# Low-rank products of a fused adaLN-FFN in three fp32r passes, their factors split by GpSimd, and two output tiles between z and the close

## The reference

```python
q = quantise(x)                      # 8 threshold groups, 64 levels, dequantised again
gates = softmax over the top 2 of 4 of (q @ router_w.T)
x = x + sum_e gates[e] * 4 * (q @ A[e].T) @ B[e].T          # 4 experts of rank 16
y = x @ W.T + 0.5 * (x @ lora_A[label[b]]) @ lora_B_w.T      # rank 32, one of 5 per batch
z = y @ kernel + bias + (y @ A_eff[b].T) @ B_eff[b].T + (y @ A_shared.T) @ B_shared.T
return x + z                         # A_eff, B_eff: 16 adapters mixed by gate[b], rank 32
```

## Time and profile before

| | |
|---|---|
| three timed runs | 505.6, 509.23, 509.37 us, median 509.23 |
| the profiled execution | 506.32 us, its span 504.5 us |
| busy: PE, weight load, DVE, ACT, POOL | 468.8, 407.4, 393.5, 364.7, 7.8 us |
| mean granted TensorE clock | 0.992 of 2.4 GHz |
| matmul records | 2968 |

### The profile page before, as it was taken

How to read it: one execution, slowest core, us unless ns; L and a number is a source line. 1 busy time by engine, 2 the same in 40 slices (tenths; PEclk the granted TensorE clock), 3 DMA queues, 4 the chain that set the end, 5 groups by cost and what they waited for, 6 DMA issues and landing times.

```text
span 504.5 us, 7250 instructions
## 1 busy us (share of the span) xinstructions
PE 468.8 (93%) x2968; PEld 407.4 (81%) x2968; DVE 393.5 (78%) x380; ACT 364.7 (72%) x330; POOL 7.8 (2%) x12
## 2 busy tenths in 40 slices
PE   3779998997798999999999999999999799989897
PEld 3654786786566888789898998998998798978896
DVE  0596578977998989949769989799699993899610
ACT  4856977857679579765779799795899778579002
POOL 0000000001000001000000000000000000000000
PEclk9999999999899999999999999999999989999999
DMA  8955641212432236410413414312413103101102
GB/s 289 388 212 164 221 137 53 54 51 53 135 94 56 70 119 149 168 46 1 129 30 124 146 54 125 106 53 73 149 61 128 48 24 127 53 2 42 43 1 83
DMA packets 36082, 51.24 MB, mean 102 GB/s; under 512 B 27058, under 2 KB 27314, under 8 KB 33650
## 3 DMA queue, kind: packets, MB, share of 16 engines
q1 hardware_dynamic: 34898, 42.40, 26.6%
q0 software_dynamic: 1152, 8.39, 4.6%
HBM read 40.03 MB, written 10.49 MB: 100 GB/s over the span
## 4 chain that ended last, share of the span: by engine, by line
PE 62%; DVE 18%; ACT 10%; issue 7%; DMA 2%; ACTq 0%; DVEq 0%; POOLq 0%
PE bank L887 11%; PE bank L889 11%; PE bank L888 11%; DVE val L572 7%; PE bank L899 5%; PE bank L807 5%; PE bank L781 4%; ACT val L381 4%; DVE val L555 3%; ACT level L370 3%; DVE inside L565 3%; PE bank L846 2%; PE bank L850 2%; PE bank L847 2%; PE bank L803 2%
## 5 line engine op out<-in xcount | busy, mean ns | idle before, releaser
L887 PE MATMUL bank<-x_hi,p_hi 128*128 128x256 f32 x512 | 154.4, 302 | 0.0
L381 ACT ACTIVATE val<-level,shift,par 128x2048 f32<-128x2048 int16 x64 | 133.9, 2092 | 21.0 <-DVE val L572 21.0
L889 PE MATMUL bank<-x_hi,p_lo 128*128 128x256 f32 x512 | 145.1, 283 | 0.0
L888 PE MATMUL bank<-x_lo,p_hi 128*128 128x256 f32 x512 | 145.1, 283 | 0.0
L572 DVE COPY_PREDICATED val<-inside,val 128x2048 f32<-128x2048 uint8 x56 | 141.9, 2534 | 0.3
L370 ACT ACTIVATE level<-xq,inv 128x2048 int16<-128x2048 f32 x64 | 127.8, 1997 | 0.4
L555 DVE TENSOR_SCALAR val<-val,width,unshift 128x2048 f32<-128x2048 f32 x64 | 86.2, 1348 | 40.5 <-ACT val L381 40.0
L887 PEld LDWEIGHTS bank<-x_hi,p_hi 128*128 128x128 f32 x512 | 98.3, 192 | 5.7 <-issue 4.6
L888 PEld LDWEIGHTS bank<-x_lo,p_hi 128*128 128x128 f32 x512 | 98.4, 192 | 1.1
L889 PEld LDWEIGHTS bank<-x_hi,p_lo 128*128 128x128 f32 x512 | 98.3, 192 | 0.0
L565 DVE TENSOR_SCALAR inside<-absx,thr 128x2048 uint8<-128x2048 f32 x56 | 71.3, 1286 | 1.8 <-ACT absx L362 1.8
(11 more groups left out here) (83 smaller groups left out, 470.0 us busy)
## 6 DMA issues: line engine op xcount, KB each, us to landing
xq<-xt_in POOLq DMA_DIRECT2D x8, 1024.0 KB, 5.9
wst<-w_in SPq DMA_DIRECT2D x16, 512.0 KB, 3.5
xs<-xt_in SPq DMA_DIRECT2D x8, 1024.0 KB, 6.3
out_t<-ost SPq DMA_DIRECT2D x16, 512.0 KB, 3.0
la<-la_in SPq DMA_DIRECT2D x4, 512.0 KB, 7.2
kst<-k_in SPq DMA_DIRECT2D x4, 512.0 KB, 12.7
lb<-lb_in SPq DMA_DIRECT2D x1, 2048.0 KB, 21.7
kst<-k_in SPq DMA_DIRECT2D x1, 2048.0 KB, 8.0
```

The lines of the kernel that those rows point to most:

```text
L381: nc.scalar.activation(val[:, turn(c, g)], level[:, g % 2], ACT.Relu, bias=shift[:, g:g + 1], scale=par[:, 1, g:g + 1]).then_inc(raised, 1)
L887: mm(o, p_hi[:, h, k, at:at + P], x_hi[:, s, k], start=k == 0, stop=False)
L888: mm(o, p_hi[:, h, k, at:at + P], x_lo[:, s, k], start=False, stop=False)
L889: mm(o, p_lo[:, h, k, at:at + P], x_hi[:, s, k], start=False, stop=False)
```

## The change

- **Three passes for z.** bu_product (bet*ub, unchanged, fp32) is now a function of its own, and z_begin is 8 times three fp32r matmuls, ub_hi*x_hi + ub_hi*x_lo + ub_lo*x_hi, with the x_hi and x_lo that the tiles use. So it waits for x_lo and ub_lo. The place is behind tile j = 5 (ZAT), where it was 4; for batch 0 z_begin stands behind the products of bet with P (L867 to L869), where it was ahead of them.
- **Three passes for each close.** tb_hi*z_hi + tb_hi*z_lo + tb_lo*z_hi in place of tb*zt.
- **GpSimd splits for each batch.** adapters_split: ub_hi and ub_lo, 128x512 each; z_split: z_hi and z_lo, 128x256 each. In its order adapters_split(b+1) stands ahead of z_split(b). ub has one buffer instead of two, and SP's adapters(b) waits for the split and the bu product of the batch before.
- **The rows of tb are split once.** DVE makes t_lo (8 instructions of 64x512), the two v_lo rows and two bp_lo rows; the lo part of t goes through DRAM too; ACT writes the bp rows once (2 instructions less), and two DMAs copy them to the second slot.
- **The xq loads** go from POOL's queue to ACT's.
- **The schedule.** z_end(z) follows tile ZEND[z], now q = 5, 13, 21, 30, 41, 50, 61 for batches 1 to 7, and the close follows two tiles later where six banks allow it: CLOSE is q = 0, 8, 16, 24, 32, 43, 52, 61 (before 0, 8, 16, 24, 32, 41, 50, 61). XAT is (0, 2), was (1, 3).

```diff
+    XAT, ZAT = (0, 2), 5
+    MID, RANK, GATE, TURN, OUT_AT = {}, {}, {}, {}, []
+    ZEND, CLOSE = [], []
     for c, d in enumerate(DONE):
         mid_at, rank_at, gate_at, turn_at, out_at = LAGS[c]
         MID[d + mid_at], RANK[d + rank_at], GATE[d + gate_at], TURN[d + turn_at] = c, c, c, c
-
-        OUT[d + out_at if c < ZSLOTS else max(d + out_at, STEPS + (c - ZSLOTS + 1) * KT)] = c
-    OUT = {c: at for at, c in OUT.items()}
-    OUT_AT = OUT
-    OUT = {at: c for c, at in OUT_AT.items()}
-
-    XAT, ZAT = (1, 3), 4
-
-
-    CLOSE = [0 if OUT_AT[b] < STEPS + b * KT else max(1, OUT_AT[b] - STEPS - b * KT) for b in range(BATCH)]
-
-    ZOUT = [b * KT + (CLOSE[b] + 1 if CLOSE[b] else 0) for b in range(BATCH)]
+        OUT_AT.append(max(d + out_at, STEPS + ZEND[c - ZSLOTS] + 2 if c >= ZSLOTS else 0))
+
+        ZEND.append(max(OUT_AT[c] - STEPS, (c - 1) * KT + ZAT))
+        CLOSE.append(min(max(ZEND[c] + 2, c * KT), c * KT + CRING - 1))
+        assert CLOSE[c] >= ZEND[c]
+    OUT = {at: c for c, at in enumerate(OUT_AT)}
+    ZOUT = [0] + [z + 1 for z in ZEND[1:]]
     LAG = 2
-    TAKE = [max(q + LAG, ZOUT[q // KT]) for q in range(BATCH * KT)]
+    TAKE = [max(q + LAG, CLOSE[q // KT] + 1) for q in range(BATCH * KT)]
...
-            for c in range(BATCH):
-                if c == 1:
-                    pool.wait_ge(bw_in, 16)
-                if c >= 2:
-                    pool.wait_ge(levels_made, (c - 1) * G)
-                    pool.wait_ge(abs_made, c - 1)
-                pool.dma_start(xq[:, c % 2], x_v[c]).then_inc(xq_in[c % 2], 16)
+            def adapters_split(b):
+                pool.wait_ge(ub_in, 32 * (b + 1))
+                if b:
+                    pool.wait_ge(z_read, b)
+                nc.gpsimd.tensor_copy(ub_hi, ub).then_inc(ub_hi_made, 1)
+                pool.wait_ge(ub_hi_made, b + 1)
+                nc.gpsimd.tensor_tensor(ub_lo, ub, ub_hi.bitcast(F32), ALU.subtract).then_inc(ub_lo_made, 1)
+
+            def z_split(b):
+                pool.wait_ge(zt_made, b + 1)
+                pool.wait_ge(mgt_made, b + 1)
+                if b >= 2:
+                    pool.wait_ge(ofull, STEPS + (b - 1) * KT)
+                nc.gpsimd.tensor_copy(z_hi[:, b % 2], zt[:, b % ZSLOTS]).then_inc(z_hi_made, 1)
+                pool.wait_ge(z_hi_made, b + 1)
+                nc.gpsimd.tensor_tensor(z_lo[:, b % 2], zt[:, b % ZSLOTS], z_hi[:, b % 2].bitcast(F32), ALU.subtract).then_inc(z_lo_made, 1)
+
+            adapters_split(0)
+            for b in range(BATCH):
+                if b + 1 < BATCH:
+                    adapters_split(b + 1)
+                z_split(b)
...
-                sp.dma_start(t_dram[g * RG:(g + 1) * RG].rearrange("r b d -> (r b) d"), tst[0:2 * R, g % 2]).then_inc(t_stored[g % 2], 16)
+                sp.dma_start(t_dram[0][g * RG:(g + 1) * RG].rearrange("r b d -> (r b) d"), tb_hi[0:2 * R, g % 2].bitcast(F32)).then_inc(t_stored[g % 2], 16)
+                sp.wait_ge(t_lo_made, 2 * (g + 1))
+                sp.dma_start(t_dram[1][g * RG:(g + 1) * RG].rearrange("r b d -> (r b) d"), t_lo[:, g % 2].bitcast(F32)).then_inc(t_stored[g % 2], 16)
 
             def adapters(b):
-                s = b % 2
-                sp.dma_start(ub[:, s, :, 0:R], u_dram[b]).then_inc(ub_in[s], 16)
-                sp.dma_start(ub[:, s, :, R:2 * R], a["al"][bass.ds(label[b], 1)].rearrange("o p k r -> p (o k) r")).then_inc(ub_in[s], 16)
+                if b:
+                    sp.wait_ge(ub_lo_made, b)
+                    sp.wait_ge(bufull, b)
+                sp.dma_start(ub[:, :, 0:R], u_dram[b]).then_inc(ub_in, 16)
+                sp.dma_start(ub[:, :, R:2 * R], a["al"][bass.ds(label[b], 1)].rearrange("o p k r -> p (o k) r")).then_inc(ub_in, 16)
...
             sp.wait_ge(w_hi_made, STEPS)
             sp.wait_ge(w_lo_made, STEPS)
             sp.dma_start(bet, a["bet"]).then_inc(bet_in, 16)
             sp.wait_ge(ofull, STEPS - 1)
             sp.dma_start(xs, x_v[0]).then_inc(xs_in, 16)
+            adapters(1)
 
             def xs_load(b):
                 sp.wait_ge(x_lo_made, b * XPARTS)
-                sp.wait_ge(z_read, b)
                 sp.dma_start(xs, x_v[b]).then_inc(xs_in, 16)
-                if b + 1 < BATCH:
-                    adapters(b + 1)
-
+
+            sp.wait_ge(bp_made, HALVES)
+            sp.wait_ge(bp_lo_made, HALVES)
+            sp.dma_start(tb_hi[2 * R:P, 1].bitcast(F32), tb_hi[2 * R:P, 0].bitcast(F32)).then_inc(bp_moved, 16)
+            sp.dma_start(tb_lo[2 * R:P, 1].bitcast(F32), tb_lo[2 * R:P, 0].bitcast(F32)).then_inc(bp_moved, 16)
             xs_load(1)
             for b in range(BATCH):
                 for h in range(HALVES):
...
                     sp.dma_start(out_t[b, :, half], ost[:, half]).then_inc(out_stored[h], 16)
                     if h == 0 and b + 2 < BATCH:
                         xs_load(b + 2)
+                        adapters(b + 2)
...
+                if g + 1 == G and c + 2 < BATCH:
+                    act.wait_ge(levels_made, (c + 1) * G)
+                    act.wait_ge(abs_made, c + 1)
+                    act.dma_start(xq[:, c % 2], x_v[c + 2]).then_inc(xq_in[c % 2], 16)
...
+            def v_lo_rows(h):
+                dve.wait_ge(v_made, h + 1)
+                at = slice(h * HALF, (h + 1) * HALF)
+                nc.vector.scalar_tensor_tensor(tb_lo[3 * R:4 * R, 0, at], misc[3 * R:4 * R], LORA1, tb_hi[3 * R:4 * R, 0, at].bitcast(F32),
+                                               ALU.mult, ALU.subtract).then_inc(v_lo_made, 1)
+
+            def t_lo_rows(n):
+                g, h = divmod(n, HALVES)
+                at = slice(h * HALF, (h + 1) * HALF)
+                dve.wait_ge(t_made, n + 1)
+                if g >= 2 and h == 0:
+                    dve.wait_ge(t_stored[g % 2], 32 * (g // 2))
+                nc.vector.tensor_tensor(t_lo[:, g % 2, at], obank[n % RING][0:2 * R], tb_hi[0:2 * R, g % 2, at].bitcast(F32),
+                                        ALU.subtract).then_inc(t_lo_made, 1)
+
+            def bp_lo_rows():
+                for h in range(HALVES):
+                    at = slice(h * HALF, (h + 1) * HALF)
+                    dve.wait_ge(bp_made, h + 1)
+                    nc.vector.tensor_tensor(tb_lo[2 * R:P, 0, at], sbank[h][ER:2 * ER], tb_hi[2 * R:P, 0, at].bitcast(F32),
+                                            ALU.subtract).then_inc(bp_lo_made, 1)
...
-            quant(*ORDER[3])
+            v_lo_rows(0)
+            for n in range(NG * HALVES):
+                t_lo_rows(n)
+                if n == NG - 1:
+                    quant(*ORDER[3])
...
                     k_add(1, n - 1)
                 if n == KT:
                     kp_lo_part(1)
+                    v_lo_rows(1)
                 if n and n + 1 < STEPS:
                     weight_lo(n + 1)
                 if n:
...
             p_out(STEPS - 1)
             for p in range(XPARTS):
                 x_part(0, p)
+            bp_lo_rows()
...
-                    pe.wait_ge(t_made, n - RING + 1)
+                    pe.wait_ge(t_lo_made, n - RING + 1)
...
-            def z_begin(c):
-
-                t = c % 2
-                pe.wait_ge(ub_in[t], 32 * (c // 2 + 1))
+            def bu_product(c):
+
+                pe.wait_ge(ub_in, 32 * (c + 1))
                 pe.wait_ge(bet_in, 16)
                 if c:
                     pe.wait_ge(zt_made, c)
                     pe.wait_ge(bu_made, c)
                 for k in range(KT):
-                    last = mm(zbank[ER:2 * ER, TOK:TOK + 2 * R], bet[:, k, ER:2 * ER], ub[:, t, k], start=k == 0, stop=k == KT - 1)
+                    last = mm(zbank[ER:2 * ER, TOK:TOK + 2 * R], bet[:, k, ER:2 * ER], ub[:, k], start=k == 0, stop=k == KT - 1)
                 last.then_inc(bufull, 1)
-                pe.wait_ge(xs_in, 16 * (c + 1))
+
+            def z_begin(c):
+
+                t = c % 2
+                pe.wait_ge(ub_lo_made, c + 1)
+                pe.wait_ge(x_lo_made, (c + 1) * XPARTS)
                 for k in range(KT):
-                    last = mm(zbank[0:2 * R, 0:TOK], ub[:, t, k], xs[:, k], start=k == 0, stop=False)
+                    mm(zbank[0:2 * R, 0:TOK], ub_hi[:, k], x_hi[:, t, k], start=k == 0, stop=False)
+                    mm(zbank[0:2 * R, 0:TOK], ub_hi[:, k], x_lo[:, t, k], start=False, stop=False)
+                    last = mm(zbank[0:2 * R, 0:TOK], ub_lo[:, k], x_hi[:, t, k], start=False, stop=False)
                 last.then_inc(z_read, 1)
...
-            z_begin(0)
+            bu_product(0)
...
+            z_begin(0)
             z_end(0)
...
-                    if j == CLOSE[b]:
-                        if j:
-                            z_end(b)
-                        pe.wait_ge(zt_made, b + 1)
-                        pe.wait_ge(tb_in[s], 16 * (b // 2 + 1))
-                        pe.wait_ge(v_moved, 32)
-                        pe.wait_ge(bp_made, HALVES * min(b + 1, 2))
-
```

(23 more changed lines are left out.)

74 lines of the change are left out of this document (42 added, 32 removed).

## The result

The changed kernel is slower: 525.28 us, median of four runs (520.15 to 535.81), beside 507.42 for the kernel before (504.83 to 509.37). The ratio is 1.028, 95% interval 1.023 to 1.033, taken without its two longest runs; with them the medians lie 3.5% apart. The profiled execution took 520.15 us, its span 518.2 against 504.5: 13.7 us more, where I had forecast 2.9.

The account below looks back on a forecast made before the run. PE was taken to set the pace up to mid(6), DVE from there to 474.50, then PE again. The terms summed to +2.9 us: 509.2 for the profiled execution, 512.0 against the median, range 503 to 527.

Parts of the forecast that it names:

- PE's price of the passes: In PE's closes and z products: three fp32r passes save 0.07 us a tile and 0.6 us a batch.
- 9.8: PE up to mid(6): -9.8 us from 47 closes, z of batches 1 to 6, and batch 5's 2.75 us wait gone.
- C: Rival on PE's passes: switching stationary factors keeps close at 0.43 and z at 3.5 us; +10, 522 us; chance 0.06.
- The P loop's terms: Before the batch loop: +1 us for ACT waiting on t's second store, +1.5 for DVE's second v_lo row.
- The start: Start of the batch loop: PE stands for bet_lo until 207.96, then bet products and z follow; +2.5 us.
- z_split(0), +0.5: Batch 0's close: z_split(0) stands behind adapters_split(1), with one 2.9 us tile to hide both; +0.5 us.
- z_split in batches 1 to 4, +4: Closes of batches 1 to 4 wait for GpSimd's z_lo: +1 us each, +4 in sum, between 0 and 12.
- DVE held by GpSimd, +2.5: From 431 to 475, where DVE is full, adapters_split(7) and z_split(6) hold it: +2.5 us, between 0 and 5.
- The tail, +0.7: Behind mid(7): eight closes give -0.6 us, z_split(7) bare between z_end(7) and the close +1.3; sum +0.7.
- B: Rival at four closes and DVE behind mid(6): GpSimd becomes the bound, 3 us per close; 525 us; chance 0.24.
- D: Rival at mid(3) and mid(5): PE waits there for DVE and closes hide; sum 0 to +3; with forecast 0.52.

Follow-up runs that it names:

- after_again: Second profile and second series of the changed kernel, nothing altered; profiled span 519.4 us, six runs from 518.8 to 533.5 us.
- e1_pool_order: Changed kernel with z_split(b) ahead of adapters_split(b+1) in GpSimd's program; ratio 1.017 to the kernel before.
- h1_dve_start: Changed kernel with batch 1's x load ahead of the bp DMAs on SP, and bp_lo rows behind DVE's first quantiser group; ratio 1.015 to the kernel before.
- e2_fill: Changed kernel with dummy matmuls in three PE waits: ahead of bet_lo, tile 0's close and mid(7); median 512.6 us, ratio 1.009 to the kernel before.
- h4_dve_yields: Changed kernel with found waits mended (GpSimd order, first close, start moves, lo products last, mid(7) later), plus DVE waiting for z_lo in batches 1 to 6; 503.5 us.
- b2_mid_later: Kernel before, fp32 products kept, with closes of batches 5 and 6 two tiles later and mid(7) one tile later; median 498.13 us.
- b1_late_close: Kernel before, fp32 products kept, with only the closes of batches 5 and 6 two tiles later; ratio 0.993 to the kernel before.
- e3_close2: Changed kernel with tiles 0, 1 and 2 closed together behind tile 2; median 514.64 us, ratio 1.013 to the kernel before.

## Why the prediction was right in its range and wrong in its size

The stated range, 503 to 527, holds the measured 525.28, and the forecast itself, 512.0, was 13 us short. By mid(6) the terms came to -0.3 and PE was 7.7 later; for DVE behind mid(6) I had +2.5 and it was -0.55; for the tail +0.7 and it was +6.9. That the range held is in good part luck: its upper end was priced from another mechanism.

**PE's price of the passes: right.** A close steps the tile from 3.30 to 3.23, z's products take 258.19 to 260.97 = 2.8 instead of 3.6, and PE gained 1.2 us in batch 2 (tiles 16 to 24), by a forecast of 8 x 0.07 + 0.6 = 1.16. From tile 2 to tile 46 it gained 6.4 net of 3.65 at tile 32 and 0.46 at a mid: 10.5 gross, where I had 9.8, and C is out. The 9.8 had the 2.75 us wait but not the 1.5 of clock behind it, so the passes themselves gave a little less than I said.

**The P loop's terms: right in sum.** bu starts at 206.28, 2.35 later than before, by +1 +1.5 = 2.5. Of this 0.6 was there when the second half began, 155.30 instead of 154.69. The rest is in this profile another slow stretch, 156.6 to 160.1 at 0.51, behind a wait of 1.83 for kp_lo; in after_again, which has none there, PE waits 1.17 for w_lo instead, as the term had it.

**The start: the wait right, the clock missing.** The gap ahead of the bet products is 3.24 (I had 3.06), and costs 1.7 more behind it.

**z_split(0), +0.5: the first wrong step.** It measured 5.71 of wait and 1.6 of clock. I had named the order, adapters_split(1) ahead of z_split(0), and then hid both behind one tile at undisturbed prices. e1_pool_order, which mends the order alone, has 3.7 us less of this wait; h1_dve_start, which takes DVE's quantiser group away from beside it, has 5.0 less. The two overlap: either mends most of it. The group was there because the bp_lo rows had pushed it. Those rows, which make DVE wait 9.95 us, I had priced nowhere.

**z_split in batches 1 to 4, +4: right in sum by luck.** 1.96 us of wait and 1.7 of clock, which the term did not have, at tile 32; nothing at 8 and 16, where ub_lo and z_lo took 1.29 and 0.73, and nothing at 24, though z_lo took 2.95 there.

**DVE held by GpSimd, +2.5: too much.** From mid(6)'s result to the last finish DVE took 43.5 us (437.86 to 481.35), less than the 44.05 before, because a wait of 1.16 us for ACT was gone; tensor_scalar and compare beside z_split(6) were 0.6 longer. adapters_split(7), which I had put into this stretch, ran at 434.24 to 436.20, in DVE's wait for mid(6). Where all four splits do fall into it, in e1_pool_order, DVE's 38 instructions take 46.9 us in sum, 1.8 more than before.

**The tail, +0.7: the second wrong step.** It measured 6.9, beside a wait at mid(7) that grew by 2.2: 4.5 behind mid(7) and 1.6 behind the last close are clock, 1.3 the bare z_split (that term was right), less 0.6 for the closes. I had written that what PE gains ahead of mid(7) counts nothing. It counts less than nothing: the gain turned 1.35 us of wait into 3.56, and the longer wait cost the clock.

**What the sum left out.** Of the 10.8 us between forecast and profile, 9.5 are the clock behind five waits (11, less 1.5 that the kernel before had paid), for which the prediction has no term at all, and 5.2 the wait at tile 0 beyond its +0.5; DVE behind mid(6) gave 3.0 back and the other terms together 1. e2_fill shows 6.5 of the clock by filling waits; the 3.0 at tile 32 and at the last close went in the same run without that. The median of 525 is B's number, and that is luck, not B's mechanism: GpSimd made one wait of 2 us at the four closes and not four of 3, and DVE was not the loser. D was right in its mechanism (in e1_pool_order PE waits for DVE's finish at mid(3), mid(5), mid(6) and mid(7), 0.49, 1.02, 0.70 and 4.90) and wrong in its price, since behind the longest of these waits comes the slow stretch.

**Where the gain of three passes went.** With every wait mended (h4_dve_yields) PE is 2.8 us further at tile 57 than with the schedule alone (b2_mid_later), yet DVE's last finish stands at 466.45 against 466.19, and the end is 3.1 later. The schedule of z and close was the useful part of the change: alone (b1_late_close) it gives 0.7%, and 1.7% with mid(7) a tile later, which the change did not have. It needs no split.

**Open.** Why DVE lets GpSimd in at once in one execution and after 12 us in the next is not settled. Nor is whether the changed kernel's own long runs are such casts: in its six runs of a second series (after_again), 518.8, 520.4, 521.4 and then 532.3, 532.5, 533.5, with the kernel before between 504.2 and 513.5 beside them, they form a group 12 us off, as h1_dve_start's did. So the spread is not the chip's, which both kernels would share. e1_pool_order, e2_fill and e3_close2 have such runs too (524.96 and 529.42, 526.16, 526.85); the twelve of h4_dve_yields, where DVE lets GpSimd in, have none, which speaks for the casts. But both profiles of the changed kernel fell on short runs, and their longest split in the batch loop is 3.2 us.

## What to carry to other kernels

Price a wait of TensorE with what comes behind it: look at the granted clock of the few microseconds after each gap in the trace, and when a gap can't be removed, try to move a tile of real work into it. When an engine ahead of TensorE sets the end, making TensorE faster lengthens that gap, so see to the gap first. Don't hang a short GpSimd instruction on the critical path beside a densely filled DVE: price it at its longest, not at its undisturbed time.

## What the runs showed of the hardware

- **The clock behind a gap.** In all fourteen traces, from 60 us on, every stretch at 1.2 GHz lies at a wait of PE of over 1.7 us or behind the program's end. Gaps of 1.66 us and less kept the clock (1.35 and 1.44 in the kernel before, 1.61 at tile 8 in e3_close2). All of 2.73 and more lost it (2.75 in the kernel before, 3.24, 5.71 and 3.56 in the changed one). Between 1.73 and 2.72 both occur: 1.96 ahead of tile 32's close gave 0.61 in the changed kernel and 1.94 gave 1.00 in e2_fill; 1.73 at the last close gave 0.54 in the changed kernel and 1.00 in e2_fill; 2.72 at 121.48 in the kernel before gave 1.00, and the same 2.72 at 121.98 in the changed one 0.57 from 122 to 126. What decides there is not shown.
- **GpSimd beside DVE.** A 128x256 cast takes 0.40 alone, and took 6.9 and 11.7 beside an unbroken row of DVE instructions; a 128x512 cast took 0.61 and 12.0. The Trainium skill (SBUF — State Buffer, Who interferes with whom) has whoever comes first keep the shared ports for a whole instruction; these rows go beyond it, over eight instructions. In two kernels with the same order on GpSimd the cast of z_hi of batch 5 took 0.95 (e1_pool_order) and 6.90 (h2_order_fill). DVE pays too: its tensor_scalar took 2.28 beside ub_lo and 1.34 alone.
- **Undisturbed prices.** ub_lo, a 512-column difference on GpSimd, took 1.29, where I had taken 0.6; the estimate by the Trainium skill's table (GPSIMD Engine Reference, Performance versus the Vector engine), 1.1, was nearer. The first instruction of its kind took 6.08 at 198.80, hidden as said.
